# Gate and up products ahead of the preceding unit's down products in a mixture-of-experts kernel on one Trainium2 core

## The reference: what is computed

```python
h   = relu(((n * x + x.sum(axis=1)) * relu(cond @ W3 + b3)) @ W2 + b2)        # conditioning
scores = softmax(h @ gate_w.T)                                                 # 64 experts
topk_w, topk_i = top_k(scores, 6)             # each expert takes its first 64 tokens
buf = zeros((64, 64 + 1, 512)).at[expert, slot].set(h[token])
g, u = buf @ w_gate, buf @ w_up                                                # 512 -> 352
y    = (silu(g) * u) @ w_down                                                  # 352 -> 512
moe  = (y[expert, slot] * weight).summed over a token's 6 experts
shared = silu(h @ sw_gate) * (h @ sw_up) @ sw_down                             # 512 -> 704 -> 512
out  = x + moe + shared
```

## Time and profile before

| | us |
|---|---|
| Time, median of 3 runs | 1211.96 |
| Lowest and highest | 1211.59 and 1214.84 |
| The profiled execution, its own time | 1211.44 |
| Its span, first to last instruction | 1209.6 |
| TensorE busy (matmuls) | 1204.5 |
| VectorE busy | 857.4 |
| ScalarE busy | 329.9 |
| GpSimd busy | 272.9 |

### The profile page before, as it was taken

The page is one execution under the profiler, slowest core; times in us unless marked ns, Lnnn a source line. Parts: engine busy times, 40 slices in busy tenths (PEclk is TensorE's granted clock), DMA queues, the critical chain, the costliest instruction groups (busy, mean ns, idle before and its releaser), DMA issues.

```text
span 1209.6 us, 15909 instructions
## 1 busy us (share of the span) xinstructions
PE 1204.5 (100%) x5705; PEld 889.3 (74%) x5705; DVE 857.4 (71%) x1868; ACT 329.9 (27%) x631; POOL 272.9 (23%) x246
## 2 busy tenths in 40 slices
PE   9999999999999999999999999999999999999998
PEld 8888888888888888888866666666666666666666
DVE  7998989988888898886656555664655664655652
ACT  4454243434324353343111111110111201111111
POOL 0000000000000000000136245263463553543421
PEclk9999999999999999999999999999999999999999
DMA  9946444372643626246767988989989889899863
GB/s 220 223 111 192 96 135 118 92 179 52 179 103 85 174 75 158 56 141 200 244 222 248 333 278 271 338 280 276 338 260 327 299 284 307 292 304 301 275 145 87
DMA packets 158999, 250.91 MB, mean 207 GB/s; under 512 B 22664, under 2 KB 93704, under 8 KB 157768
## 3 DMA queue, kind: packets, MB, share of 16 engines
q1 hardware_dynamic: 142528, 222.22, 58.3%
q0 software_dynamic: 14048, 25.18, 10.5%
q10 hardware_dynamic: 2344, 2.50, 0.7%
HBM read 197.14 MB, written 61.10 MB: 213 GB/s over the span
## 4 chain that ended last, share of the span: by engine, by line
PE 95%; DVE 3%; issue 0%; ACT 0%; DMA 0%; DVEq 0%; ACTq 0%
PE bank L1509 23%; PE bank L1510 22%; PE bank L1511 22%; PE bank L1713 13%; PE bank L1728 7%; PE bank L1535 2%; PE bank L1632 1%; PE bank L1631 1%; PE bank L1569 1%; PE bank L1567 1%; PE bank L1580 1%; PE bank L1638 0%; DVE x L951 0%; DVE xpart L955 0%; DVE x L968 0%
## 5 line engine op out<-in xcount | busy, mean ns | idle before, releaser
L1509 PE MATMUL bank<-hh,gu 128*128 128x512 f32 x704 | 278.0, 395 | 0.0
L1510 PE MATMUL bank<-hl,gu 128*128 128x512 f32 x704 | 274.2, 390 | 0.0
L1511 PE MATMUL bank<-hh,gu 128*128 128x512 f32 x704 | 274.1, 389 | 0.0
L629 POOL DMA_INDIRECT hg<-table,idx_quarter x128 | 126.5, 988 | 643.5 <-DVE idx_hi L1391 594.0
L1509 PEld LDWEIGHTS bank<-hh,gu 128*128 128x128 f32 x704 | 132.2, 188 | 39.1 <-issue 12.8
L1511 PEld LDWEIGHTS bank<-hh,gu 128*128 128x128 f32 x704 | 132.2, 188 | 27.8
L1510 PEld LDWEIGHTS bank<-hl,gu 128*128 128x128 f32 x704 | 132.2, 188 | 26.2
L697 ACT ACTIVATE ah<-prod 128x512 fp32r<-128x512 f32 x96 | 60.6, 632 | 302.6 <-DVE prod L1051 287.2
L1468 DVE STREAM_TRANSPOSE eactT<-eact 32x96 f32<-32x96 f32 (+1 forms) x512 | 133.9, 261 | 7.9
L1509 PE MATMUL bank<-sdh,ah 128*128 128x512 f32 x320 | 125.9, 393 | 0.0
L1510 PE MATMUL bank<-sdl,ah 128*128 128x512 f32 x320 | 124.6, 390 | 0.0
(11 more groups left out here) (132 smaller groups left out, 1672.8 us busy)
## 6 DMA issues: line engine op xcount, KB each, us to landing
wg<-in_L_ffn_w_gate_dram SPq DMA_DIRECT2D x64, 704.0 KB
wu<-in_L_ffn_w_up_dram SPq DMA_DIRECT2D x64, 704.0 KB
wd<-in_L_ffn_w_down_dram SPq DMA_DIRECT2D x64, 512.0 KB
table<-hrow SPq DMA_DIRECT2D x64, 256.0 KB, 4.3
x<-in_x_dram SPq DMA_DIRECT2D x60, 256.0 KB, 6.8
wd<-in_L_ffn_w_down_dram SPq DMA_DIRECT2D x64, 192.0 KB
out_dram<-outst SPq DMA_DIRECT2D x35, 256.0 KB
outst<-in_x_dram SPq DMA_DIRECT2D x32, 256.0 KB, 3.5
```

The lines of the kernel that those rows point to most:

```text
L629: nc.gpsimd.indirect_dma_start(out=hg[p % 3][:, b, :], out_offset=None, in_=quarters, in_offset=bass.IndirectOffsetOnAxis(ap=idx_quarter[: ...
L1509: nc.tensor.matmul(o, st_h, mv_h, start=first_mm, stop=False)
L1510: nc.tensor.matmul(o, st_h, mv_l, start=False, stop=False)
L1511: return nc.tensor.matmul(o, st_l, mv_h, start=False, stop=last_mm)
```

## The change

In every "experts" piece three engines do their parts in another order. TensorE does the gate and up products of pair p first, and the down product of pair p - 1 last. SyncE asks for gate and up of pair p + 2 first and for down of pair p last. VectorE does `product_expert` ahead of `scale_y`. Nothing is added or left out, and ScalarE's and GpSimd's programs stay as they are.

```diff
@@ block.sync, second stage
                 if kind == "gate_up" and j == 1 and n + 1 < 2 * ND:
                     load_hT(n + 1 - ND)
-                if kind == "experts" and 0 < n < NP:
-                    load_down(n)
                 if kind == "experts" and n + 2 < NP:
                     load_gate(n + 2)
                     load_up(n + 2)
+                if kind == "experts" and 0 < n < NP:
+                    load_down(n)
@@ block.vector, second stage
                 if kind == "experts":
+                    if n < NP:
+                        product_expert(n)
                     scale_y(n - 1)
                     if n < NP:
-                        product_expert(n)
                         turn_act(n, (0, 1))
@@ block.tensor
             def experts(p):
+                expert_gate_up(p)
                 expert_down(p - 1)
-                expert_gate_up(p)
```

## The result

| | before | after |
|---|---|---|
| Time, median, us | 1211.78 | 1229.38 |
| Lowest and highest | 1211.57 and 1214.84 | 1228.25 and 1233.31 |
| The profiled execution, its own time | 1211.44 | 1228.25 |
| Its span | 1209.6 | 1226.5 |

The ratio is 1.0146, 95% interval 1.0134 to 1.0159. The forecast was 1216.0 and its range ended at 1222.0: the sign was right, the size far off, and the time lies outside the range.

A forecast was written before the change was run, and what follows sets the result against it. TensorE was taken to bound the kernel, so only added waits would count. Switching 0, down weights 4.0, scatters 0 and VectorE and ScalarE 0 on 1211.96 gave 1216.0 us, with an 80% range of 1212.2 to 1222.

The forecast's parts named there:

- What bounds the kernel, and the sign: TensorE, busy 1204.5 of 1209.6 us: an added wait lengthens the time, and only switching could be won.
- Switching: TensorE's borders between kinds of matmul: the new order costs 0, from -1.6 to +1.6 us.
- The down weights: Single-buffered down loads, now queued behind gate and up, make TensorE's down products wait: 4.0 us, 1.5 to 9.3.
- The near ones: Some six of 29 units, like unit 21, whose down weights land close to their need; one counted, 0.5 us.
- VectorE and ScalarE: Transposes behind product_expert and scale_y end about 1 us later: cost 0, up to 1 if a tile's last split is caught.
- signs of being wrong: Profile after: idle time before gate products, granted clock below 1.00, waits in nearly every unit, or at shared tiles.
- The scatters: GpSimd's scatter chain ends up to 4.8 us later, with 2.2 of room: 0 beside the weights, 2.6 alone.
- Rival (d): Scatter chain sets the end: at 7 us of lag the fourth tile waits 4.8 us, 1216.8; chance 0.09.
- Rival (c): TensorE's clock falls at the two waits of 2 us and more, each costing 2 more: 1220 us; chance 0.06.
- Rival (b): Weight queue falls behind for good, most units wait for down weights, 29 x 0.5 = 15 us: 1226; chance 0.07.

The follow-up runs named there:

- both mends and small adds: Changed kernel with down weights asked for first, next pair's rows transposed before eact's second half, and GpSimd's adds cut to 64 of 512 columns: 1211.66 us.
- both mends: Changed kernel with down weights asked for first again and VectorE transposing the next pair's rows before the second half of eact: 1219.31 us.
- rows first: Changed kernel with VectorE transposing the next pair's rows (hgt) before the second half of eact, down loads still last: 1224.92 us.

## Why the prediction was wrong

- **What bounds the kernel, and the sign: right.** TensorE is busy throughout, nothing could be won but switching, and every wait adds its length.
- **Switching, 0: right.** The up to down border costs nothing beyond its products' time, and the kernel with both mends and small adds has the span before.
- **The down weights, 4.0 (1.5 to 9.3): right in mechanism and places, too small in size.** Measured 7.1. Unit 13 lost 3.6 against 2.2, unit 9 1.6 against 1.3. The near ones were units 5 and 27, not 21. The byte counts were kinder than the prediction allowed for. At unit 13's need, 849.73, the queue had moved 3.82 MB since its unit's first load, not 4.03; and at unit 9's, 774.73, it had moved 4.48, more than the unit's 4.33, and still the weights came 1.4 us later (`q1 hardware_dynamic: 1066, 3.82, 63.3%` from 831.7 on, and `q1 hardware_dynamic: 1353, 4.48, 66.6%` from 755.7 on). The count takes in the load of `h`, asked for right behind the down weights, and what follows. So the bytes of the queue say that the need comes close to the landing, which held, but not by how much.
- **"VectorE and ScalarE ... 0, and up to 1": this is the step that failed.** Measured 7.4 us, as much as the weights, of which 6.1 in seven units that show it in every kernel with TensorE's new order and the rows behind `eact`. The prediction followed VectorE's transposes to "about 1 us later" and asked only whether the shared tiles would wait for them. It never asked who reads `hgt` and when. The reader is the first product of a unit now, 2.63 us earlier than before, and in seven units the room before was 1.5 to 2.5, less than that move alone. VectorE's own delay, which the prediction did look at, adds 0.8 in two of them. The trace before had it all, 765.70 against 768.17 in unit 9. The prediction listed idle time before the gate products among its signs of being wrong, and this is the one that came. The kernel with TensorE's part alone shows the wait (1220.88), the one with VectorE's part alone does not have it.
- **The scatters, 0 beside the weights, up to 2.6 without them: right.** In the changed kernel the chain has even caught up: the last scatter starts at 1208.43, 9.0 us behind unit 32, where it was 10.6 behind before. That was not expected, since the chain was said to have no slack. With both mends it is 4.2 us later behind unit 32 than before, within the 4.8 forecast, and the fourth tile waits 2.0. Rival (d), a lag of more than 4.8, is in no trace.
- **Rival (c), the clock, was given 0.06 and came true once:** behind 3.4 us of standing still, 1.8 us, about what it was priced at (2). What was wrong was to hold it against the forecast as a case of its own, where it is a part of the price of a long wait.
- **Rival (b), the queue behind in most units:** not in this change, and very much so when the loads are reordered without the products. The argument against it, that each wait gives the queue time, is what the loads alone disproved.

With the waits for `hgt` at their measured size in place of the 0, the forecast would have been 1211.96 + 4.0 + 7.4 = 1223.4; with the weights and the clock at their measured sizes too, the sum is 1227.7 on the profiled execution's time of 1211.44.

## What to carry to other kernels

When work is moved forward on the engine that bounds the kernel, list every buffer that it reads, and take from the trace when each was ready against when it was used: the room must be more than the move, for each of them and in the unit where it is least. Where a buffer is single and its load is asked for only when the last use is over, what stands ahead in the queue is part of the loop, and a delay comes back every round. And count a wait of 3 us or more on TensorE as longer than it is, by a stretch at half clock: it cost 1.8 us behind 3.4 here.

## What the runs showed of the hardware that was not expected

The clock falls behind a single wait in the midst of full work. Behind waits of 3.4 us (the changed kernel) and 4.0 (rows first) there was a slow stretch, behind 1.4 (unit 9 of the changed kernel) none. In the kernel with both mends it came behind only 1.8 to 2.0 us. Its length alone doesn't tell what a wait will do: in the kernel with the loads alone all waits from 2.9 us up had a slow stretch at their end or behind them, and of ten waits between 2.1 and 2.7 two had one (2.5 us, ending at 877.10) and eight had none (2.7 us, ending at 759.53). The Trainium skill (TensorE: Matmul & The Clock Gate, Part 1) says that idleness puts the clock back to half; these runs agree with that, the down product taking 4.49 us in place of 2.80 at a granted clock of 0.66.
